# A mamba unit's exponent as one bf16 product of copied rows, and the gate's plus one on ScalarE

## The reference, cut to what matters

```python
zxbcdt = x @ in_w
z   = zxbcdt[..., :D_INNER]                      # 256 columns
xBC = conv(zxbcdt[..., D_INNER:D_INNER + 512])   # 4 taps along the tokens
xBC = silu(xBC)                                  # xs (256), Bm (128), Cm (128)
dt  = softplus(zxbcdt[..., -NHEADS:] + dt_bias)  # 4 heads
S   = segsum(dt * A);  L = exp(S)                # masked above the diagonal
Y   = einsum(Cm, Bm, L, xs * dt) + C @ state * exp(cumsum(dt * A))
state = decay * state + B^T (xs * dt)
y   = (Y + D * xs) * silu(z)
y   = y * rsqrt(mean(y * y) + 1e-5) * norm_w
out = sum over experts of (y @ out_w) * softmax(x @ router_w)
```

## Time and profile before

| | |
|---|---|
| time, median of 3 runs | 1970.87 us |
| profiled execution, its own time (span) | 2081.0 us |
| mamba block in the trace | 303 to 1061 us |
| its loop, first to last `begin` | 374.48 to 978.46 us |
| granted TensorE clock, whole span | 0.887 of full |

### The profile page before, as it was taken

One profiled execution on the slowest core, in us unless ns is written; L12 is line 12 of the kernel. 1 busy time (PEld: TensorE's weight loads), 2 busy tenths in 40 slices (PEclk: granted clock), 3 DMA queues, 4 the chain that ended last, 5 costly groups with the idle time before them and its releaser, 6 DMA issues. The chain is left out here.

```text
span 2081.0 us, 37179 instructions
## 1 busy us (share of the span) xinstructions
PE 1653.0 (79%) x10974; PEld 1391.3 (67%) x11039; DVE 1350.5 (65%) x3003; ACT 864.4 (42%) x1914; POOL 1051.1 (51%) x1188
## 2 busy tenths in 40 slices
PE   6889954899999999999978898538993776477763
PEld 4569941688888888888845698528881555366762
DVE  4534467899999999999645354574663665633435
ACT  2212226555555555555422122125662454333341
POOL 2135532577777777777621356344425551555552
PEclk9989955999999999999979999659996898589896
DMA  6001130000000000000050011502211410011114
GB/s 218 1 23 36 37 87 0 1 1 1 1 1 1 1 1 1 1 1 1 1 172 5 21 34 38 180 9 55 59 51 40 122 39 21 15 38 40 35 38 137
DMA packets 68556, 81.59 MB, mean 39 GB/s; under 512 B 25489, under 2 KB 40753, under 8 KB 68417
## 3 DMA queue, kind: packets, MB, share of 16 engines
q1 hardware_dynamic: 54432, 51.46, 8.0%
q0 software_dynamic: 13856, 28.40, 5.2%
q10 hardware_dynamic: 128, 0.02, 0.0%
HBM read 54.93 MB, written 24.90 MB: 38 GB/s over the span
## 5 line engine op out<-in xcount | busy, mean ns | idle before, releaser
L865 PE MATMUL ps<-w,inner_slot 128*128 x1760 | 257.5, 291 | 58.4 <-DVE y L956 33.0
L853 PE MATMUL ps<-gT,w_slot 128*128 128x128 f32 x1760 | 255.7, 292 | 31.2 <-ACT gT L887 21.2
L865 PEld LDWEIGHTS ps<-w,inner_slot 128*128 128x128 f32 x1760 | 228.4, 202 | 75.0 <-issue 73.9
L853 PEld LDWEIGHTS ps<-gT,w_slot 128*128 128x128 f32 x1760 | 233.3, 206 | 39.3 <-issue 29.0
L816 POOL DMA_INDIRECT y_rows<-y,slot_row x149 | 153.1, 1027 | 209.2 <-DVE y L950 110.5
L1800 DVE SCALAR_TENSOR_TENSOR cv<-ps,cw,cv 128x1021 f32<-128x1021 f32 (+2 forms) x192 | 245.0, 1276 | 8.5 <-ACT cv L1694 5.9
L810 POOL DMA_INDIRECT rows_in<-xn_rows,slot_token x188 | 186.9, 994 | 125.4 <-PE ps L841 74.2
L933 DVE TENSOR_TENSOR hb<-ps,b 128x512 f32<-128x512 f32 x142 | 98.2, 691 | 202.8 <-PE ps L853 124.5
L1972 POOL TENSOR_TENSOR y<-t,sz 128x256 f32<-128x256 f32 x128 | 94.7, 740 | 186.9 <-DVE t L1844 184.0
L1571 PE MATMUL ps<-xnT,win 128*128 128x512 f32 x256 | 130.1, 634 | 28.9 <-DVE cv L1800 25.5
L1620 PE MATMUL ps<-XB,LM 128*128 128x64 f32 x1024 | 142.9, 262 | 0.0
(11 more groups left out here) (299 smaller groups left out, 4172.6 us busy)
## 6 DMA issues: line engine op xcount, KB each, us to landing
w<-in_L_ffn_W SPq DMA_DIRECT2D x6, 2048.0 KB, 10.9
xn_rows<-xn SPq DMA_DIRECT2D x24, 256.0 KB
xn<-y_rows SPq DMA_DIRECT2D x24, 256.0 KB, 5.2
y_rows<-y SPq DMA_DIRECT2D x71, 64.0 KB
rows_in<-xn_rows,slot_token POOLq DMA_INDIRECT x220
y_rows<-y,slot_row POOLq DMA_INDIRECT x149
xn_rows<-rows SPq DMA_DIRECT2D x8, 256.0 KB
xnT<-y_rows SPq DMA_DIRECT2D x8, 256.0 KB, 6.1
```

Of the source, the lines that this page charges most:

```text
L853: ins = nc.tensor.matmul(h1[:, u, b * P:(b + 1) * P], w[:, b * P:(b + 1) * P], k.gT[:, r, :], start=True, stop=True)
L865: ins = nc.tensor.matmul(py[:, q % 2, :], k.inner_slot[:, q % RING, b * P:(b + 1) * P], w_dn[:, ds(e * (FB * D) + b * D, D)], start=(b == ...
```

## The change

1. **Exponent.** `pickA` and `pickQ` go. Two new tensors, `left` (8 lanes of 128 columns) and `right` (8 lanes of 512 columns), hold both sides of one product for 8 units in turn. Their constant parts (ones, and the quads of the mask) are made once by GpSimd as `left0` and `right0` and copied into all lanes by two DMAs. The parts that depend on the unit are copied from `m.rows` by SyncE: per group of 4 units, one DMA of 12 rows into `left` and four of 3 rows into `right`. Each is issued when the group before the previous one has its exponents, and TensorE waits for the five to land. A unit's exponent is then one product of 512 columns.
2. **Parts.** The three bf16 parts of a head now lie side by side (the write has a step of three elements), and the rows that are transposed and copied are 96 and not 128.
3. **Plus one.** In the loop it moves from VectorE's list to ScalarE's, behind the square, as the last instruction of the odd step.

```diff
@@ TensorE, open_unit
-                rows = m.rows[:, tile * P:(tile + 1) * P]
-                nc.tensor.matmul(bankL, rows, m.pickQ[:, e, :], start=True, stop=False, skip_group_check=True)
-                for h in range(MH):
-                    ins = nc.tensor.matmul(bankL[:, h * P:(h + 1) * P], m.pickA[:, e * MH + h, :], rows,
-                                           start=False, stop=(h == MH - 1), skip_group_check=True)
-                inc(ins, b["exponent"])
+                batch = u // GRP
+                wait(pe, pieces_in[batch % 2], (batch // 2 + 1) * (MH + 1))
+                inc(nc.tensor.matmul(bankL, m.left[:, u % HELD, :], m.right[:, u % HELD, :], start=True, stop=True),
+                    b["exponent"])
@@ ScalarE
-            inc(A.copy(m.pickQ[:, :, :].rearrange("p e (h l) -> p (e h) l", h=MH), bcast(sel[:, 1, :], 2, P)), picked)
...
-            inc(A.copy(m.pickA[:, :, :], bcast(sel[:, 0, :], 2, P)), picked)
...
                 if ok(t - 1):
                     square(t - 1)
+                if piece_of(t, 2) is not None:
+                    twice_sigmoid(piece_of(t, 2))
@@ VectorE
-            for src, first in ((acs, 0), (q, 3)):
-                for part in range(3):
-                    out = parts[:, :, (first + part) * MEH:(first + part + 1) * MEH]
+            for side, src in enumerate((acs, q)):
+                kept = parts[:, :, side * PARTS * MEH:(side + 1) * PARTS * MEH].rearrange("p t (n c) -> p t n c", c=PARTS)
+                for part in range(PARTS):
+                    out = kept[:, :, :, part]
...
-                if piece_of(t, 2) is not None:
-                    twice_sigmoid(piece_of(t, 2))
@@ SyncE, new
+                wait(sp, b["exponent"], (n - 1) * GRP)
+                sp.dma_start(m.left[0:MH * PARTS, lanes, :],
+                             m.rows[(MEH + e * MH) * PARTS:(MEH + e * MH + MH) * PARTS, tokens].rearrange("p (t l) -> p t l", l=P)
+                             ).then_inc(into, 16)
+                for h in range(MH):
+                    sp.dma_start(m.right[SUMS + h * PARTS:SUMS + (h + 1) * PARTS, lanes, h * P:(h + 1) * P],
+                                 m.rows[first + h * PARTS:first + (h + 1) * PARTS, tokens].rearrange("p (t l) -> p t l", l=P)
+                                 ).then_inc(into, 16)
...
+            wait(sp, consts, 10)
+            sp.dma_start(m.left[:, :, :], bcast(m.left0[:, :], 1, HELD)).then_inc(sides_filled.sem, 16)
+            sp.dma_start(m.right[:, :, :], bcast(m.right0[:, :], 1, HELD)).then_inc(sides_filled.sem, 16)
+            wait(sp, sides_filled, 2)
+            wait(sp, rows_copied, NG)
+            for n in range(NQ):
+                exponent_rows(n)
```

More of the change, by code:

```diff
@@ L28 @@
 ME, MH = 4, 4
+HELD = 8
 ZW, CW = 256, 512
@@ L1445, in mamba @@
         m.tri, m.identb = S("tri", [P, P]), S("identb", [P, P], BF16)
-        m.pickA, m.pickQ = S("pickA", [P, MEH, P], BF16), S("pickQ", [P, ME, MH * P], BF16)
+        m.left, m.right = S("left", [P, HELD, P], BF16), S("right", [P, HELD, MH * P], BF16)
+        m.left0, m.right0 = S("left0", [P, P], BF16), S("right0", [P, MH * P], BF16)
         m.rout = S("rout", [P, NT * ME])
@@ L1480, in mamba_units @@
     N = NT * MEH
+    PARTS = 3
+    ROWS = 2 * PARTS * MEH
+    SUMS = 32
     QUADS = 6 * MEH
@@ L1501, in mamba_units @@
     z0, ratio = (t[:, :, :].rearrange("p a n -> p (a n)") for t in (t2, carried))
-    sel = S("sel", [P, 2, MEH])
     q = m.q
     mx, sm, parts = S("mx", [P, NT]), S("sm", [P, NT]), LM[:, :, :].bitcast(BF16).rearrange("p a (t k) -> p (a t) k", k=P)
+    sides_filled = k.counter("exponent_constants_in", 16)
+    pieces_in = [k.counter(f"exponent_rows_in{r}", 16) for r in range(2)]
     parts_ready, rows_turned, rows_copied = (k.counter(f"scalars_{n}") for n in ("parts_ready", "rows_turned", "rows_copied"))
-    consts, own, to_act, acted, a_ready, sums_ready, scaled, weighed, picked = (
+    consts, own, to_act, acted, a_ready, sums_ready, scaled, weighed = (
         k.counter(f"scalars_{n}") for n in ("constants", "vector_step", "to_scalar", "scalar_step", "a_ready", "sums_ready",
-                                            "conv_scaled", "weights_scaled", "picks_copied"))
+                                            "conv_scaled", "weights_scaled"))
     lg = k.logits[:, 0:NT * NM].rearrange("p (t n) -> p t n", n=NM)
@@ L1646, in turn_rows @@
             def turn_rows():
-                wait(pe, consts, 5)
+                wait(pe, consts, 2)
                 wait(pe, parts_ready, 1)
@@ L1651, in turn_rows @@
                     for j in range(GRP):
-                        ins = nc.tensor.matmul(k.ps[:, 6 + g % 2, j * P:(j + 1) * P], parts[:, g * GRP + j, :],
+                        ins = nc.tensor.matmul(k.ps[0:ROWS, 6 + g % 2, j * P:(j + 1) * P], parts[:, g * GRP + j, 0:ROWS],
                                                m.identb[:, :], start=True, stop=True)
@@ L1666, in _ @@
             wait(pe, init, 1)
-            wait(pe, consts, 14)
             wait(pe, weighed, 1)
-            wait(pe, picked, 2)
-            wait(pe, rows_copied, NG)
+            wait(pe, sides_filled, 2)
             for t in steps:
@@ L1700, in tanh_piece, with twice_sigmoid @@
                 inc(A.activation(th[:, :], cv[:, n % 2, :], ACT.Tanh), a["tanh"])
+            def twice_sigmoid(n):
+                wait(act, a["tanh"], n + 1)
+                inc(A.activation(th[:, :], th[:, :], ACT.Identity, bias=k.ones[:, 0:1]), a["sigmoid"])
             def early_gate(n):
                 tanh_piece(n)
-                wait(act, a["tanh"], n + 1)
-                inc(A.activation(th[:, :], th[:, :], ACT.Identity, bias=k.ones[:, 0:1]), a["sigmoid"])
+                twice_sigmoid(n)
             def z_unit(u):
@@ L1742, in _ @@
             begin(1)
-            wait(act, consts, 13)
-            inc(A.copy(m.pickQ[:, :, :].rearrange("p e (h l) -> p (e h) l", h=MH), bcast(sel[:, 1, :], 2, P)), picked)
             wait(act, to_act, 3)
@@ L1758, in _ @@
                 wait(act, rows_turned, g + 1)
-                A.copy(m.rows[:, g * GRP * P:(g + 1) * GRP * P], k.ps[:, 6 + g % 2, :]).then_inc(rows_copied.sem, 1)
+                A.copy(m.rows[0:ROWS, g * GRP * P:(g + 1) * GRP * P], k.ps[0:ROWS, 6 + g % 2, :]
+                       ).then_inc(rows_copied.sem, 1)
             early_gate(3)
@@ L1801, in tap @@
                     tap_done if i < 2 else a["conv"])
-            def twice_sigmoid(n):
-                wait(dve, a["tanh"], n + 1)
-                inc(V.tensor_scalar(th[:, :], th[:, :], 1.0, None, ALU.add), a["sigmoid"])
             def gate(u):
@@ L1902, in _ @@
                 do(V.memset(first, 0.0))
-            wait(dve, consts, 3)
-            for src, first in ((acs, 0), (q, 3)):
-                for part in range(3):
-                    out = parts[:, :, (first + part) * MEH:(first + part + 1) * MEH]
+            for side, src in enumerate((acs, q)):
+                kept = parts[:, :, side * PARTS * MEH:(side + 1) * PARTS * MEH].rearrange("p t (n c) -> p t n c", c=PARTS)
+                for part in range(PARTS):
+                    out = kept[:, :, :, part]
                     do(V.tensor_copy(out, by_head(src)))
-                    if part < 2:
+                    if part < PARTS - 1:
                         do(V.tensor_tensor(by_head(src), by_head(src), out, ALU.subtract))
@@ L1938, in _, with exponent_rows @@
                     tap(piece_of(t, 1), 1)
-                if piece_of(t, 2) is not None:
-                    twice_sigmoid(piece_of(t, 2))
+        @block.sync
+        def _(sp):
+            def exponent_rows(n):
+                _, e, _, tile = unit(n * GRP)
+                into, lanes, tokens = pieces_in[n % 2].sem, slice(n * GRP % HELD, n * GRP % HELD + GRP), slice(tile * P, (tile + GRP) * P)
+                first = e * MH * PARTS
+                wait(sp, b["exponent"], (n - 1) * GRP)
[13 more added lines that the diff above has]
+                exponent_rows(n)
+            for r in range(2):
+                wait(sp, pieces_in[r], NQ // 2 * (MH + 1))
         @block.gpsimd
@@ L1989, in _ @@
             do(G.tensor_copy(m.identb[:, :], k.ident[:, :]))
[L1990 to L2003, removed]
+            right0 = heads(m.right0[:, :])
@@ new lines, in _ @@
+            do(G.memset(m.right0[:, :], 1.0))
+            do(G.affine_select(out=right0, in_=right0, compare_op=ALU.is_ge, fill=0.0, base=0,
+                               pattern=[[-PARTS, MH], [0, P]], channel_multiplier=1))
+            do(G.affine_select(out=right0, in_=right0, compare_op=ALU.is_ge, fill=0.0, base=PARTS - 1,
+                               pattern=[[PARTS, MH], [0, P]], channel_multiplier=-1))
+            do(G.affine_select(out=right0, in_=right0, compare_op=ALU.is_ge, fill=-1e30, base=4 * QUADS,
+                               pattern=[[0, MH], [1, P]], channel_multiplier=-4))
@@ L2004, in _ @@
```

(12 more changed lines are left out.)

## The result

The changed kernel takes 2000.79 us (median of 4 runs) against 1973.78 for the kernel before: a ratio of 1.0137, 95% interval 1.0116 to 1.0158. That is 27 us slower. The forecast was 1992.6, which is 21.7 slower, in a range of 1963 to 2006.

What follows compares the result with a forecast made beforehand. The prediction took TensorE's loop of waits, 10.62 us per pair, as the bound, which the plus one would replace with a silu loop of 11.03. Terms +23.9 and -2.2 gave +21.7 on 1970.9: 1992.6 us, range 1963 to 2006.

Steps and rivals of the forecast that it cites:

- Two loops of waits, 10.62 and 9.98: Mamba loop, per pair of steps: TensorE's loop of waits takes 10.62 us and sets the period, the silu loop 9.98.
- The plus one, 1.05 per pair, so 11.03: On ScalarE between square and `begin`: it lengthens the silu loop from 9.98 to 11.03 us, which becomes the period.
- The term of 0.42 x 56 = 23.5: Mamba loop: the period grows by 0.42 us in each of 56 pairs, 23.5 us in all.
- The rule on adds: Skill's rule giving plain adds to VectorE: by it the move costs for its duration, by the rows for its place.
- The plus one off VectorE, 0: VectorE in the loop: 1.18 us less work per pair is worth nothing, as VectorE then waits for ScalarE.
- One product for five, 0 in the pairs: TensorE in the 57 pairs: 0.22 us less per unit only widens waits, gain 0.
- One product for five, -2.2 after the last piece: Some 10 steps after the last piece: TensorE is the bound there, so the lighter exponent saves 2.2 us.
- 4.1 as a sign: Steps after the last piece should last 4.1 us and not 4.3 in the new trace.
- The row copies, 0: SyncE's five DMAs per 4 units, issued two groups ahead: they hide and cost 0.
- Ahead of the loop, 0: Before the loop: dropped copies and GpSimd steps against slower stepped casts, taken as 0, bounds -2 and +2 us.
- The rival of no change: GpSimd, relieved of VectorE's plus one, speeds its loop by 0.4 or more; period stays 10.62, time 1969; chance 0.15.
- the silu loop: Waits from GpSimd's silu through ScalarE's tanh, square and `begin`, then sums and gating to the next silu; 9.98 us.

Runs made afterwards that it cites:

- plus_one_only: The kernel before with only the plus one moved to ScalarE's list, the exponent left as it was; 2001.64 us, ratio 1.0136.
- plus_one_later: The changed kernel with the plus one still on ScalarE but one step later, at the end of the even step; 1976.23 us, ratio 1.0010.
- short_norm_later: The changed kernel with the loop's plus one over 768 of 1024 columns and GpSimd's norm moved to the even step behind the weighing; 1980.88 us, run once.
- product_only: The changed kernel with the plus one back on VectorE, so only the exponent's half of the change; 1976.33 us, ratio 1.0005.
- tap_first: plus_one_later with VectorE's tap 0 moved ahead of the z gate and the matrices; 1956.40 us, ratio 0.9919.
- norm_later: tap_first with GpSimd's three norm steps moved to the even step behind the weighing of X; 1947.30 us, ratio 0.9850.

## Why the prediction was right, and where it was not

- **Two loops of waits, 10.62 and 9.98.** Shown: adding the plus one to the second gives 11.06 alone (plus_one_only), taking it out of that place gives 10.60 (plus_one_later), and a shorter one shortens the period by as much (short_norm_later).
- **The plus one, 1.05 per pair, so 11.03.** It is 1.04, and pairs without a norm take 10.99. The first pair was forecast at +0.36 and measured at +0.36. What I missed is the norm: every second pair takes 11.12, 0.13 more, since GpSimd's weighing then lies beside the matrices. The term of 0.42 x 56 = 23.5 became 25.8: 0.38 x 56 = 21.4 from the plus one, a little less than forecast, and 4.4 from the norm's pairs and a few longer ones.
- **The rule on adds.** The Trainium skill, page ScalarE: Activation LUTs, "Rules for kernel authors", gives plain adds to VectorE. The kernel as changed agrees with it (+27 us). In plus_one_later, with the same add on ScalarE, nothing is lost (ratio 1.0010). The add takes 1.18 on VectorE and 1.13 to 1.17 on ScalarE, so its duration does not explain the 27 us, and its place does.
- **The plus one off VectorE, 0.** Shown by plus_one_only and plus_one_later: VectorE's busy share fell by 10 and more points with no gain.
- **One product for five, 0 in the pairs.** Shown by product_only.
- **One product for five, -2.2 after the last piece.** Wrong, though the measured part is -2.5. The step that failed is the reading "TensorE is the bound (9.95 busy of 10)". In product_only, which has the one product, this part takes 82.8 and not less. Steps there last 4.31 or 4.32 us before and after, where the forecast named 4.1 as a sign. TensorE in the changed kernel:

```profile
1024.21 0.38 PE L1604 MATMUL ps<-right,left 128*128 128x512 bf16 x1
1024.64 0.41 PE L1632 MATMUL ps<-ident,y 128*128 128x128 f32 x2
...
1028.96 0.41 PE L1632 MATMUL ps<-ident,y 128*128 128x128 f32 x2
```

and VectorE between:

```profile
1027.34 0.42 DVE L1833 TENSOR_TENSOR state<-ps,carried 128x256 f32<-128x256 f32 x1 [1.18 <-PE ps L1624]
...
1028.47 0.34 DVE L1852 SCALAR_TENSOR_TENSOR x<-ps,gain,x 128x128 f32<-128x128 f32 x1
```

  From turn to state 2.70, to the addition 1.13, to the next turn 0.49: a loop of 4.32 that the product is not in. 0.43 lie between product and turn, 0.21 of them empty, and no idle time is printed because the product's modelled end, 0.38 long, covers nearly all of them. The kernel before had the same loop beside a list of 4.31, so both looked full. I had warned of modelled ends in the prediction and then leaned on a busy share.
- **The row copies, 0.** Shown by product_only. In the changed kernel SyncE's rows show 0.78 us for issuing the copy into `left` and 2.94 for the four into `right`, 3.8 from the first to the last, per group of 22 us.
- **Ahead of the loop, 0.** Measured +0.1. The casts with a step take 0.60 and not 0.43.
- **The rival of no change** (the silu loop shrinks when GpSimd is relieved) fell: GpSimd's decay in that place did fall from 1.06 to 0.61, but the tanh waits 1.99 as before, and the silu stays at 2.36.

The forecast of +21.7 against +23.8 in the block is right in its mechanism. Its tail term was right in size by luck. Of the 8.2 us between 1992.6 and 2000.8, 2.9 are the kernel before, which stands at 1973.78 here and at 1970.87 in the forecast, and 5.3 are the change.

## What to carry to other kernels

Two engines at 98% and 96% may both be held by a chain that returns to itself. Add up start to start along each such chain between two like instructions: the longest sum is the period, and the slack of the second longest is all that an instruction placed in it may cost. Before an instruction moves to an idler engine, ask which chain its new place belongs to; a step later it may be free. A saving on a busy engine is worth nothing until the chains are shorter than its list. Then measure it again, as here, where it rose from 0 to 7 us in the block.

## What was not expected of the hardware

**VectorE beside GpSimd.** The matrices, which read two tensors of SBUF, take 0.69 to 0.72 us in an even step without a norm, and 0.83 to 1.05 where GpSimd's decay or weighing lies beside them (1.00 to 1.02 in tap_first's pairs with a norm, 0.69 in the others, which is the 0.32 between 10.50 and 10.18). The Trainium skill, page SBUF — State Buffer, "Who interferes with whom", says that a VectorE instruction with two SBUF inputs contends with a GpSimd one that reads SBUF. The runs agree, and moving the norm gave 4.0 us in one kernel and 9.4 in another (block of tap_first 740.2, of norm_later 730.8).

**The clock at the end.** The 2.5 us that the last part got shorter are the granted clock. At the end of the block come closing rounds, in which a unit is only turned, multiplied by out_w and added to x. The last full step ahead of them, from turn to turn, in the kernel before:

```profile
1038.79 0.44 PE L1628 MATMUL ps<-ident,y 128*128 128x128 f32 x2 [1.46 <-DVE x L1851]
...
1044.76 0.41 PE L1628 MATMUL ps<-ident,y 128*128 128x128 f32 x2 [1.25 <-DVE x L1851]
```

and the same step in the changed kernel, with the first closing round behind it:

```profile
1050.94 0.41 PE L1632 MATMUL ps<-ident,y 128*128 128x128 f32 x2 [1.68 <-DVE x L1852]
...
1055.26 0.41 PE L1632 MATMUL ps<-ident,y 128*128 128x128 f32 x2 [1.25 <-DVE x L1852]
...
1057.38 0.41 PE L1632 MATMUL ps<-ident,y 128*128 128x128 f32 x2 [0.54 <-DVE x L1852]
```

The step takes 5.97 us before and 4.32 after. In the kernel before, windows of 1 us give the lower level (0.50 to 0.52 of full) from 1039 to 1042, the full one from 1043 to 1045, and the lower one again from 1046 on. In the changed kernel the level stays full until near 1059, behind the first two closing rounds. A closing round in the kernel before:

```profile
1050.09 0.66 PE L1628 MATMUL ps<-ident,y 128*128 128x128 f32 x2 [0.54 <-DVE x L1851]
...
1052.96 0.66 PE L1628 MATMUL ps<-ident,y 128*128 128x128 f32 x2 [0.54 <-DVE x L1851]
```

A round takes 2.87 us at the lower level and 2.12 at the full one. From that step's first turn to the last turn are 5.97 + 2.45 + 4 x 2.88 = 19.9 us before and 4.32 + 2 x 2.12 + 3 x 2.88 = 17.2 after, 2.7 less, of which a slightly longer stretch ahead takes back 0.2.

The same step lasts 5.97 or 5.98 in all three kernels with pairs of 10.61 (before, product_only, plus_one_later; last part 82.65 to 82.9) and 4.31 or 4.32 in the nine others (79.0 to 81.6). Tap_first and norm_later are among these, so it does not hang on the plus one's place ahead of `begin`. Why the level falls earlier in the three is open, and no run tests it by itself. An idle stretch of TensorE just ahead does not decide it: the 1.46 us before the turn at 1038.79 came with a fall, the 1.68 before 1050.94 did not.
